# A vision-transformer block on one core: the first patch projection in six loads, four of its six parts in split precision, and the attention matrices loaded in two pieces

## The reference, cut to what matters

```python
patches = _patchify(x, 16)                     # 32 images: 36 patches of 768 numbers each
h = concatenate([cls, einsum('bnf,df->bnd', patches, W) + b], axis=1) + pos_enc    # 32 x 37 x 256
h = h + attn(layernorm(h))                     # Q and K products with V_b, V_t, W_b, W_t; running sums over the
                                               # tokens; U_b, U_t and Wo behind them
h = h + moe(layernorm(h))                      # router over 8 experts, 2 chosen; 256 -> 1024 -> gelu -> 256
```

## Time and profile before

| what | value |
|---|---|
| median of three runs | 158.75 us (158.63 to 159.4) |
| the profiled execution | 158.79 us |
| its span, first to last instruction | 157.0 us |
| outside the span | 1.79 us |
| TensorE busy | 147.5 us, 94% |
| VectorE, ScalarE, GpSimd busy | 105.6, 82.5 and 51.0 us |
| granted TensorE clock, mean | 0.993 of full speed |

### The profile page before, as it was taken

How to read it: one execution, slowest core, us unless ns; L and a number is a source line. 1 busy time by engine, 2 the same in 40 slices (tenths; PEclk the granted TensorE clock), 3 DMA queues, 4 the chain that set the end, 5 groups by cost and what they waited for, 6 DMA issues and landing times.

```text
span 157.0 us, 2952 instructions
## 1 busy us (share of the span) xinstructions
PE 147.5 (94%) x982; PEld 138.7 (88%) x982; DVE 105.6 (67%) x330; ACT 82.5 (53%) x210; POOL 51.0 (32%) x55
## 2 busy tenths in 40 slices
PE   7999999999999979999999999999999999999950
PEld 6559999899689768899799999999999999999940
DVE  0075985769796899981498679579486694885610
ACT  3224653734317998857058266574683666737100
POOL 6002000505430000005437267084381761504361
PEclk9999999999999999999999999999999999999997
DMA  5999960089501445651206898879868988600422
GB/s 165 417 430 427 398 231 0 0 266 370 216 4 39 138 160 179 202 176 29 73 0 125 268 285 237 250 168 325 267 138 263 258 260 259 134 3 1 48 25 24
DMA packets 16978, 28.46 MB, mean 181 GB/s; under 512 B 1133, under 2 KB 13591, under 8 KB 16585
## 3 DMA queue, kind: packets, MB, share of 16 engines
q1 hardware_dynamic: 14505, 25.49, 47.5%
q0 software_dynamic: 2464, 2.86, 10.7%
HBM read 24.21 MB, written 4.14 MB: 181 GB/s over the span
## 4 chain that ended last, share of the span: by engine, by line
PE 78%; ACT 6%; DVE 5%; issue 3%; POOL 3%; DMA 2%; POOLq 1%; DVEq 0%
PE ps L1312 24%; PE ps L1347 12%; PE ps L1145 6%; PE ps L1236 6%; PE ps L1253 5%; PE ps L1349 5%; ACT xn L569 2%; PE ps L1178 2%; PE ps L1357 2%; PE ps L1157 2%; PE ps L1324 2%; DMA rows_in<-xrows,src_row 2%; PE ps L1274 2%; PE ps L1299 2%; ACT xn L578 2%
## 5 line engine op out<-in xcount | busy, mean ns | idle before, releaser
L510 POOL DMA_INDIRECT out_rows<-out_s,dst_row x16 | 23.7, 1483 | 37.9 <-ACT out_s L695 31.6
L671 ACT ACTIVATE first_t<-ps,b_cur 128x186 f32<-128x186 f32 x64 | 23.0, 413 | 23.4 <-PE ps L1312 21.9
L1347 PE MATMUL ps<-hid_hl,split 128*128 128x372 f32 x96 | 29.0, 368 | 0.0
L1349 PE MATMUL ps<-hid_hl,split 128*128 128x186 f32 x96 | 24.0, 250 | 0.0
L1312 PE MATMUL ps<-first_t,patch_t 128*128 128x186 f32 x128 | 21.7, 322 | 0.2 <-DVE first_t L977 0.2
L990 DVE CAST hid_hl<-first_t 128x372 fp32r<-128x372 f32 x28 | 10.9, 388 | 16.0 <-ACT first_t L671 15.8
L1312 PEld LDWEIGHTS ps<-first_t,patch_t 128*128 128x128 f32 x128 | 20.1, 190 | 0.5 <-issue 0.5
L495 POOL DMA_INDIRECT rows_in<-xrows,src_row x14 | 15.8, 1125 | 10.8 <-DVE src_row L958 6.9
L535 ACT ACTIVATE split<-patch_t 128x512 fp32r<-128x512 f32 (+2 forms) x28 | 14.4, 579 | 8.4 <-DMA patch_t<-patches 5.2
L1349 PEld LDWEIGHTS ps<-hid_hl,split 128*128 128x128 f32 x96 | 18.4, 191 | 0.0
L1347 PEld LDWEIGHTS ps<-hid_hl,split 128*128 128x128 f32 x96 | 18.0, 188 | 0.0
(11 more groups left out here) (181 smaller groups left out, 269.5 us busy)
## 6 DMA issues: line engine op xcount, KB each, us to landing
patch_t<-w SPq DMA_DIRECT2D x8, 1024.0 KB, 5.3
att<-w SPq DMA_DIRECT2D x3, 1024.0 KB, 6.7
h_t<-w SPq DMA_DIRECT2D x3, 1024.0 KB, 6.0
w_even<-w SPq DMA_DIRECT2D x2, 1024.0 KB, 16.9
att<-attn SPq DMA_DIRECT2D x1, 1280.0 KB, 8.6
patch_t<-patches SPq DMA_DIRECT2D x1, 1188.0 KB, 13.3
patch_t<-patches SPq DMA_DIRECT2D x1, 1080.0 KB, 10.8
first_t<-first SPq DMA_DIRECT2D x1, 978.0 KB, 6.2
```

The source lines that it names most:

```text
L510: pool.indirect_dma_start(out=out[:, :], out_offset=bass.IndirectOffsetOnAxis(ap=dst_row[0:SIZES[s], c:c + 1], axis=0), in_=out_s[q][0:SIZ ...
L671: ins = act.activation(hid[:, f, :], bank(pair)[:, (f % 2) * SL:(f % 2 + 1) * SL], ACT.Gelu, bias=b1_cur[q][:, f:f + 1])
L1347: pe.matmul(dst[:, 0:2 * SL], w2_h[q][:, f, cols], hid_hl[:, f].rearrange("p a s -> p (a s)"), start=f == 0, stop=False)
L1349: ins = pe.matmul(dst[:, 0:SL], w2_l[q][:, f, cols], hid_hl[:, f, 0], start=False, stop=f == KF - 1)
```

## The change: what it does

`first` is loaded in six pieces, one for each part. The first two parts (`WHOLE` = 2) are still multiplied in fp32. The last four are multiplied as the second and third groups are, by three fp32r products each, so ScalarE now makes for each of them a high copy of the weight and one of the patches (into `patch_h`, which the second group uses next), VectorE makes the patches' low parts, and GpSimd, no longer VectorE, makes the weight's low parts. The matrices of `att` are put in another order, and the two that `uw` needs (Wo and U) are loaded ahead of patch group B_, the others behind the constants. `mac` moves on TensorE behind the second projection, and into another place in PSUM; on ScalarE it moves behind the first normalisation.

```diff
-PIECES = [(0, 1), (1, 3), (3, KP)]
+WHOLE = 2
-A_WQ, A_WK, A_WO, A_V, A_W, A_U, A_X = layout(KD * D, KD * D, KD * D, *(4 * [KD * 2 * R]))
+A_WO, A_U, A_WQ, A_WK, A_V, A_W, A_X = layout(KD * D, KD * 2 * R, KD * D, KD * D, *(3 * [KD * 2 * R]))
-        UNITS = [("proj", A, 0), ("mac", 0, 2), ("uw", 0, 1), ("norm1", A, 0), ("proj", B_, 3), ("norm1", B_, 3),
+        UNITS = [("proj", A, 0), ("uw", 0, 1), ("norm1", A, 0), ("proj", B_, 3), ("mac", 0, 1), ("norm1", B_, 3),
-        ACT_ORDER = [("mac", 0), ("root1", A), ("norm1", A), ("xn_high", A), ("m_high", 0), ("root1", B_), ("norm1", B_),
+        ACT_ORDER = [("root1", A), ("norm1", A), ("mac", 0), ("m_high", 0), ("xn_high", A), ("root1", B_), ("norm1", B_),
...
+            for k in range(KP):
+                sp.dma_start(first_t[:, k], first[:, k * w:(k + 1) * w]).then_inc(first_in[k], 16)
             sp.dma_start(vecs[:, :], vectors).then_inc(vec_in, 16)
-            sp.dma_start(att[:, :], attn).then_inc(attn_in, 16)
+            sp.dma_start(att[:, 0:A_U.stop], attn[:, 0:A_U.stop]).then_inc(out_attn_in, 16)
...
                 if g == 1:
                     sp.dma_start(cst[:, :], const).then_inc(const_in, 16)
+                    sp.dma_start(att[:, A_U.stop:], attn[:, A_U.stop:]).then_inc(attn_in, 16)
...
             pool.memset(at_p[:, NT - 1], 0.0).then_inc(pool_set, 1)
+
+            for i, (a, b) in enumerate([(k, k + 1) for k in range(WHOLE, KP)] + [(0, WHOLE)]):
+                pool.wait_ge(tok_high, i + 1)
+                pool.tensor_tensor(tok_l[:, a:b], tok_wt[:, a:b], tok_h[:, a:b], ALU.subtract).then_inc(tok_split, 1)
...
-            for i, (a, b) in enumerate(PIECES):
-                act.wait_ge(first_in[i], 16)
-                copy(tok_h[:, a:b], tok_wt[:, a:b]).then_inc(tok_high, 1)
+            for k in range(WHOLE, KP):
+                act.wait_ge(first_in[k], 16)
+                copy(tok_h[:, k], tok_wt[:, k]).then_inc(tok_high, 1)
+                copy(patch_h[:, k, 0:FIRST], first_t[:, k, D:]).then_inc(first_high, 1)
+            for k in range(WHOLE):
+                act.wait_ge(first_in[k], 16)
+            copy(tok_h[:, 0:WHOLE], tok_wt[:, 0:WHOLE]).then_inc(tok_high, 1)
...
+                    if g == SPLIT[0] and k == 0:
+                        act.wait_ge(psum_filled, PLACE["proj", A] + 1)
...
-            for i, (a, b) in enumerate(PIECES):
-                dve.wait_ge(tok_high, i + 1)
-                dve.tensor_tensor(tok_l[:, a:b], tok_wt[:, a:b], tok_h[:, a:b], ALU.subtract).then_inc(tok_split, 1)
+            for k in range(WHOLE, KP):
+                dve.wait_ge(first_high, k - WHOLE + 1)
+                dve.tensor_tensor(patch_l[:, k, 0:FIRST], first_t[:, k, D:], patch_h[:, k, 0:FIRST], ALU.subtract
+                                  ).then_inc(first_split, 1)
...
+                        for k in range(WHOLE, KP):
+                            pe.wait_ge(tok_high, k - WHOLE + 1)
+                            pe.wait_ge(first_high, k - WHOLE + 1)
+                            for m, (w, x) in enumerate(((tok_h, patch_h), (tok_l, patch_h), (tok_h, patch_l))):
+                                if m == 1:
+                                    pe.wait_ge(tok_split, k - WHOLE + 1)
+                                if m == 2:
+                                    pe.wait_ge(first_split, k - WHOLE + 1)
+                                for d in range(KD):
+                                    ins = pe.matmul(p[:, d * 512:d * 512 + nb * NP2], w[:, k, d * 128:(d + 1) * 128],
+                                                    x[:, k, 0:FIRST], start=False, stop=k == KP - 1 and m == 2)
```

More of the change, by code:

```diff
@@ L242, in vit_block @@
         const_in, attn_in, vec_in = sem("const_in"), sem("attn_in"), sem("vec_in")
-        first_in = [sem(f"first_in{i}") for i in range(len(PIECES))]
+        out_attn_in = sem("out_attn_in")
+        first_in = [sem(f"first_in{k}") for k in range(KP)]
         patch_in = [sem(f"patch_in{g}") for g in range(len(PATCHES))]
@@ L246, in vit_block @@
         tok_high, tok_split = sem("tok_high"), sem("tok_split")
+        first_high, first_split = sem("first_high"), sem("first_split")
         patch_high, patch_split = sem("patch_high"), sem("patch_split")
@@ L383, in _ @@
         def _(sp):
-            for i, (a, b) in enumerate(PIECES):
-                w = D + FIRST
-                sp.dma_start(first_t[:, a:b].rearrange("p k d -> p (k d)"), first[:, a * w:b * w]).then_inc(first_in[i], 16)
+            w = D + FIRST
+            for k in range(KP):
+                sp.dma_start(first_t[:, k], first[:, k * w:(k + 1) * w]).then_inc(first_in[k], 16)
             sp.dma_start(vecs[:, :], vectors).then_inc(vec_in, 16)
-            sp.dma_start(att[:, :], attn).then_inc(attn_in, 16)
+            sp.dma_start(att[:, 0:A_U.stop], attn[:, 0:A_U.stop]).then_inc(out_attn_in, 16)
             for g in range(1, len(PATCHES)):
@@ L618, in _ @@
             patches_high(SPLIT[0])
+            patches_high(SPLIT[1], inside=INSIDE + 1)
             for kind, n in ACT_ORDER:
@@ L1207, in _ @@
                 if kind == "mac":
+                    pe.wait_ge(out_attn_in, 16)
                     pe.wait_ge(attn_in, 16)
@@ L1229, in _ @@
                     if n in SPLIT:
-                        pe.wait_ge(tok_split, len(PIECES))
+                        pe.wait_ge(tok_split, KP - WHOLE + 1)
                         products = [(tok_h, patch_h), (tok_l, patch_h), (tok_h, patch_l)]
@@ L1248, in _ @@
                     else:
-                        for i, (a, b) in enumerate(PIECES):
-                            pe.wait_ge(first_in[i], 16)
+                        for k in range(WHOLE):
+                            pe.wait_ge(first_in[k], 16)
                             for d in range(KD):
-                                for k in range(a, b):
-                                    ins = pe.matmul(p[:, d * 512:d * 512 + nb * NP2], tok_wt[:, k, d * 128:(d + 1) * 128],
-                                                    first_t[:, k, D:], start=k == 0, stop=k == KP - 1)
+                                pe.matmul(p[:, d * 512:d * 512 + nb * NP2], tok_wt[:, k, d * 128:(d + 1) * 128],
+                                          first_t[:, k, D:], start=k == 0, stop=False)
+                        for k in range(WHOLE, KP):
[9 more added lines that the diff above has]
+                                                    x[:, k, 0:FIRST], start=False, stop=k == KP - 1 and m == 2)
                 elif kind in ("norm1", "norm2"):
@@ L1435 @@
                    np.broadcast_to(L0_ffn_b_router, (128, NE)))
[L1436 removed]
+    attn = wide(blocks(np.asarray(L0_attn_Wo).T), blocks(wide(L0_attn_U_b, L0_attn_U_t)),
+                blocks(np.asarray(L0_attn_Wq)), blocks(np.asarray(L0_attn_Wk)),
                 blocks(wide(L0_attn_V_b, L0_attn_V_t)), blocks(wide(L0_attn_W_b, L0_attn_W_t)),
[L1438 removed]
                 blocks(np.pad(np.asarray(L0_attn_X_t), ((0, 0), (R, 0)))))
```

4 lines of the change are left out of this document (removed).

## The result

| | before | changed |
|---|---|---|
| median | 159.07 us (158.63 to 162.95, 4 runs) | 165.0 us (163.65 to 165.54, 4 runs) |
| ratio of the compared runs | | 1.037 (1.0283 to 1.0456) |
| the profiled execution, and its span | 158.79 and 157.0 us | 163.65 and 161.8 us |

The profiled execution of the changed kernel is the shortest of its four; in the other three the mean granted clock was 0.972 to 0.973 instead of its 0.984 (experiments 7 and 8).

A forecast was written before the change was run, and what follows sets the result against it. The prediction took TensorE's gapless chain from the first projection on as the bound: +5.96 for that projection's later end, -0.26 for a removed idle, +5.70 on 158.79 gave 164.5 us, range 160.0 to 167.4.

The forecast's parts named there:

- 9.90 "at best": First projection: VectorE's first low part of patches, behind `vecs`, starts at 9.33 at best and is there at 9.90.
- The clock falls behind the idle: TensorE's clock falls over a 4.8 us idle in the first projection; products then start at 0.38 us each.
- The split's own gain: First projection on TensorE: with no waits, fp32r products for 16 fp32 passes end it at 11.56, 0.76 us earlier.
- The issues, the loads of `att` and the moved `mac`: Claimed to cost nothing: six issues hidden by transfers, `uw`'s matrices landing in time, `mac` costing 1.78 us wherever it stands.
- 13.75: Earliest end of the first projection given VectorE's first low part at 9.90 and 3.80 us of products left.
- 0.56: Excess in us of the first projection's 24 passes over 24 x 0.3325, used to place the clock's rise near 4.8.
- what GpSimd does to it: First projection: TensorE waits for GpSimd's low part of the weight, there at 12.13, and idles 4.8 us.
- the reload of its code: Ahead of GpSimd's first subtraction: estimated 8.45 us from 2.95, making GpSimd ready at 11.40; middle-length case 0.50.
- that rival: Short reload of GpSimd's code or none, VectorE decides the first projection's end: 159.9 to 161.2 us, chance 0.20.
- restart, 12.2: TensorE goes on in the first projection at about 12.2, after GpSimd's first low part, with 22 products left.
- My 18.28: Forecast end of the first projection, with late GpSimd and the clock's fall: 5.96 us later than before.
- I gave back 0.26: Third projection: with `mac` moved, `m_l` is done earlier and TensorE's 0.26 us idle ahead of 31.14 goes.

The follow-up runs named there:

- experiment 7: Bridges (products nobody reads) added to the changed kernel with VectorE alone subtracting, tables behind: 160.83 us; and to the kernel before: 159.77 us.
- experiment 8: Bridges (products nobody reads) inside TensorE's wait ahead of the first `pick`: kernel before with them 158.93 us, changed kernel with them 163.98 us.
- experiment 9: Changed kernel, VectorE alone subtracting, bridges inside the `pick` wait: first kernel, `vecs` loaded second, 159.23 us; second kernel, tables behind the subtractions, 159.11 us.
- experiment 1: Changed kernel with the first projection back in fp32 throughout, six loads, `att` pieces and moved `mac` kept: 161.44 us, ratio 0.9986.
- experiment 5: Changed kernel with GpSimd's five weight subtractions given to VectorE, still behind its wait for `vecs`, plus bridges: 162.62 us, ratio 1.019.
- experiment 2: Changed kernel with VectorE's wait for `vecs` and its small tables moved behind its four low parts of patches: 160.83 us, ratio 1.0118.

## Why the number was right and one of its steps wrong

**What held.** VectorE is late behind `vecs` (I had 9.90 "at best" for its first low part). The clock falls behind the idle. The split's own gain is as worked out: 0.76 us, and 0.73 in experiment 9 (12.32 to 11.59), though that sets one profile against one, and with fp32 throughout this end alone lies between 12.06 (experiment 1) and 13.48 (experiment 7). The issues, the loads of `att` and the moved `mac` cost nothing by themselves that can be told (experiment 1). Two small slips in the sums changed nothing: 9.90 + 3.80 is 13.70, not 13.75, and the first projection took 0.48 us more than 24 passes at full clock (from 3.86 to 12.32), not 0.56.

**The step that failed is what GpSimd does to it.** I put 8.45 us for the reload of its code, an estimate halfway between two loads, had GpSimd ready at 11.40, and made TensorE wait for it. GpSimd's first subtraction started at 5.91, when ScalarE's copy was there: the reload held it up for no more than the 2.96 us of idle before and was hidden. What TensorE waited for was VectorE. The Trainium skill, GPSIMD Engine Reference, section 2.1 (Instruction dispatch), gives some 6 us for the first call to freshly loaded code; this trace shows no such price, and here the measurement decides. The prediction had named this outcome ("if instead GpSimd subtracts near 6 us, the reload costs nothing and the wait is VectorE's"), but gave it only a part of 0.20, and priced it at 159.9 to 161.2.

**Why that rival was priced too low.** It had VectorE's low part at 9.90 and no clock's fall. In the trace `vecs` landed at 8.89, 0.74 later: I had counted the bytes ahead of it, but not that six issues put its own off by 1.42. Without GpSimd the first subtraction would then have started 1.17 behind the landing (as in experiment 5), at 10.06. GpSimd's subtractions held up VectorE's small operations and so made it 11.42. I had thought of the two in each other's way only when both subtract. The Trainium skill, SBUF — State Buffer, section "Who interferes with whom", says that these two engines share one pair of ports, that copies and operations with a scalar can take it as well, and that whichever comes second waits until the other's instruction has ended. The rows agree: the copy of 10.28 ended 0.08 us behind GpSimd's subtraction, and took 0.22 where GpSimd was idle.

**How the terms met.** Against the 11.59 of the split without waits: the eight fp32 passes and the first four products ended at 8.74 (12.04 less the wait of 3.30) instead of 7.84 (7.09, and four of the 24 products that took 4.50), because both took longer in this execution, 3.76 and 1.18 us instead of 3.31 and 0.75: 0.90 (some 0.15 of it is the end of the last product, which overlaps with the next one where none waits). The idle: 3.30, of which 1.36 is GpSimd beside VectorE and 1.94 the landing of `vecs` with the tables. The 20 products at a clock that fell: 5.25 instead of 3.75, so 1.50. Sum: 17.29. I had nearly the same restart, 12.2, from a wrong cause. My 18.28 is 0.99 above it by three terms: the restart 0.16, the products that were left (22 for 4.18 instead of 20 for 3.75) 0.43, and the clock (1.90 instead of 1.50, since it fell 1.2 us behind the restart and not within the idle) 0.40.

**What came back.** I gave back 0.26. The wait for `m_l` is gone, and at 35.68 against 31.14 the loss is down from 4.97 to 4.54; but VectorE's `h_t`, for which TensorE now waits at 37.07, was late behind it, and the span is longer by 4.8.

**And the median.** My sum was made for a profiled execution: 164.5, and that came at 163.65, 0.85 below. The median lies 1.35 above it. With bridges inside the wait near 60 us most runs came back to 164 (experiment 8), so most of the 1.35 is probably the clock's second fall, for which I had no term; no profile of the changed kernel holds such a fall, so this is argued from the times and mean clocks. That the number is near is luck: the restart came out right from a wrong cause, and two errors of about a microsecond cancel.

## What to carry to other kernels

A wait in an engine's program holds up all that stands behind it: when a change gives an engine new work on the path, put that work ahead of waits that it doesn't need (here some 4 us, by moving one block of code or one load). Before a step is sped up, look at what is due next: of 0.73 us saved on TensorE 0.52 were given back at once, most of it because TensorE now came to wait for a subtraction that a GpSimd copy had always held up, and for which nothing had waited before. And where work is handed from VectorE to GpSimd to share it, count what GpSimd's subtractions add to VectorE's own small operations.

## What the runs showed of the hardware that I had not expected

- Small operations of VectorE were held up beside GpSimd's subtractions: two of 36 columns took 0.87 us instead of 0.39, a copy of 64 columns 1.10 instead of 0.22. In experiment 2, `bias_s`, 2 columns, took 1.23 instead of 0.22 and ended at 12.43, 0.03 behind GpSimd.
- TensorE's clock fell to 0.50 behind idles of 3.30 and 4.04 us, not behind one of 2.69; and in some executions also near 58 us, where the longest wait is 0.86. Bridges inside that wait left no such run in 12 of the second kernel of experiment 9, where bridges behind it had left seven (experiment 7). Why it falls there in one execution and not in the next of the same kernel stays open, as does why the rise at the start differs from one profile to another (the first 24 fp32 passes end at 12.32 in the earlier trace rows, at 13.48 in the kernel of 7).
- In the eleven kernels with six loads of one part each, 311 to 363 GB/s came in from 4 to 8 us; in the three kernels with three loads it was 420 to 428. Whether the number of loads or their order does it wasn't tried, nor how much of the 0.74 by which `vecs` landed later is this and how much its later issue.
